# Masks in one load, the gelu average on VectorE, waits reordered on ScalarE, and a new call order on five engines

## The reference

```python
xn = (x - mean(x)) / sqrt(var(x) + 1e-5)
s  = where(mask, xn @ ctx.T * 512**-0.5, -1e30)         # 128 x 128, mask by column
x1 = x + softmax(s) @ ctx
y  = (x1 - mean(x1)) / sqrt(var(x1) + 1e-5)
z  = act_quant(rms_norm(y)) @ weight_quant(w1).T + b1   # 128 x 2048
h  = gelu(silu(z))
l  = (h - mean(h)) / sqrt(var(h) + 1e-5) * g + b
out = x1 + act_quant(rms_norm(l)) @ weight_quant(w2).T + b2
```

## Time and profile before

| | us |
|---|---|
| median of three executions | 419.5 |
| the profiled execution | 421.23 |
| its span, first to last instruction | 419.4 |
| ScalarE busy | 381.8 |
| TensorE busy | 384.0 |
| VectorE busy | 365.9 |
| GpSimd busy | 271.8 |

### The profile page before, as it was taken

How to read it: one execution, slowest core, us unless ns; L and a number is a source line. 1 busy time by engine, 2 the same in 40 slices (tenths; PEclk the granted TensorE clock), 3 DMA queues, 4 the chain that set the end, 5 groups by cost and what they waited for, 6 DMA issues and landing times.

```text
span 419.4 us, 6830 instructions
## 1 busy us (share of the span) xinstructions
PE 384.0 (92%) x1878; PEld 204.7 (49%) x1878; DVE 365.9 (87%) x571; ACT 381.8 (91%) x517; POOL 271.8 (65%) x373
## 2 busy tenths in 40 slices
PE   3899988789999999999999999999999987899996
PEld 2667353535545544544555454554455532344342
DVE  5278669989998989999999999989998789999992
ACT  1497999999999999999999999999999999999960
POOL 5358488764687838764785569585468855477930
PEclk9999998899999999999999999999999996999999
DMA  7998992556755677669668757694654423083484
GB/s 278 409 312 301 359 342 69 153 162 142 211 147 131 188 193 184 103 189 204 155 169 249 190 166 148 199 222 107 174 135 106 91 63 63 2 200 102 87 214 128
DMA packets 110389, 73.87 MB, mean 176 GB/s; under 512 B 87048, under 2 KB 87056, under 8 KB 109584
## 3 DMA queue, kind: packets, MB, share of 16 engines
q1 hardware_dynamic: 110352, 73.43, 65.1%
HBM read 44.05 MB, written 8.39 MB: 125 GB/s over the span
## 4 chain that ended last, share of the span: by engine, by line
issue 25%; ACT 21%; DVE 19%; PE 17%; POOL 13%; DMA 4%; SPq 1%; DVEq 0%; POOLq 0%; ACTq 0%
ACT junk_v L1212 6%; DVE hid L1981 5%; DVE hid L1972 5%; PE z L624 4%; PE acc L649 4%; ACT hid L1201 3%; ACT hid L1207 3%; POOL hid L1618 3%; PE ba L574 3%; ACT junk_l L1223 2%; POOL rstd L1607 2%; DVE am L1986 2%; POOL xc L1563 2%; DVE st L1900 1%; DMA hid<-in_w2T_dram 1%
## 5 line engine op out<-in xcount | busy, mean ns | idle before, releaser
L624 PE MATMUL z<-w1q,q1T 128*128 128x512 f16 x512 | 124.0, 386 | 3.3 <-ACT hid L1201 3.1
L649 PE MATMUL acc<-w2q,q2T 128*128 128x512 f16 x512 | 117.4, 379 | 0.4 <-DMA q2T<-hid 0.4
L1981 DVE SCALAR_TENSOR_TENSOR hid<-hid,rstd,beta 128x2048 f32<-128x2048 f32 x32 | 76.8, 2402 | 6.2 <-POOL rstd L1607 5.9
L624 PEld LDWEIGHTS z<-w1q,q1T 128*128 128x128 f16 x512 | 49.9, 99 | 65.6 <-ACT hid L1201 9.7
L1972 DVE SCALAR_TENSOR_TENSOR hid<-hid,nmu,gain 128x2048 f32<-128x2048 f32 x32 | 79.3, 2480 | 0.4 <-POOL nmu L1599 0.3
L649 PEld LDWEIGHTS acc<-w2q,q2T 128*128 128x128 f16 x512 | 49.8, 98 | 58.2 <-issue 0.9
L1986 DVE TENSOR_REDUCE am<-hid 128x1 f32<-128x2049 f32 x32 | 72.5, 2269 | 0.1
L1201 ACT ACTIVATE hid<-z,fac 128x1024 f32<-128x1024 f32 x64 | 70.7, 1119 | 1.6 <-PE z L629 1.4
L1223 ACT ACTIVATE junk_l<-hid 128x2050 bf16<-128x2050 f32 x32 | 61.1, 1910 | 4.1 <-DVE hid L1981 4.0
L1618 POOL TENSOR_SCALAR hid<-hid,kq 128x2048 f16<-128x2048 f32 x30 | 60.9, 2031 | 4.6 <-DVE kq L1993 3.1
L1212 ACT ACTIVATE junk_v<-hid,gsum 128x2048 bf16<-128x2048 f32 x32 | 63.7, 1990 | 0.1
(11 more groups left out here) (105 smaller groups left out, 572.2 us busy)
## 6 DMA issues: line engine op xcount, KB each, us to landing
ctxT<-in_ctxT_dram SPq DMA_DIRECT2D x32, 256.0 KB, 3.5
xs<-in_x_dram SPq DMA_DIRECT2D x32, 256.0 KB, 3.9
xT<-in_xT_dram SPq DMA_DIRECT2D x32, 256.0 KB, 3.6
ctx<-in_ctx_dram SPq DMA_DIRECT2D x32, 256.0 KB, 3.4
out_dram<-xs SPq DMA_DIRECT2D x32, 256.0 KB, 3.0
hid<-in_w1T_dram SPq DMA_DIRECT2D x4, 1024.0 KB, 10.2
hid<-in_w2T_dram SPq DMA_DIRECT2D x4, 1024.0 KB, 7.8
gain<-in_g_dram SPq DMA_DIRECT2D x1, 1024.0 KB, 11.1
```

The source lines that it names most:

```text
L624: pe.matmul(z_ps[h][:, c * CH:(c + 1) * CH], q1T[:, t % 4, k, :], w1q[:, k, f0:f0 + CH], start=(k == 0), stop=False)
L649: mm = pe.matmul(a, q2T[:, t % 2, c, :], w2q[:, c, :], start=False, stop=(c == FC - 1))
L1981: dve.scalar_tensor_tensor(out=hh, in0=hh, scalar=rstd[:, t:t + 1], in1=beta[:, :], op0=ALU.mult, op1=ALU.add).then_inc(s_l, 1)
```

## The change

Masks: one load of 32 x 128 bytes and one conversion; row t of the mask is picked by multiplying with column t of the identity, broadcast over 128 columns. The matrix of ones is gone.

```diff
-        mask = sb("mask", [1, 2, G, P], U8)
-        maskb = sb("maskb", [P, 2, G, P], BF16)
+        mask = sb("mask", [NT, P], U8)
+        maskb = sb("maskb", [P, P], BF16)
...
+            def load_mask():
+                sp.dma_start(mask[:, :], mask_in[:, :]).then_inc(s_mask, 16)
...
                 if t == 0:
-                    pe.wait_ge(s_const, 1)
-                pe.wait_ge(s_maskb, t // G + 1)
-                pe.matmul(score_ps, ones_b[:, :], maskb[:, t // G % 2, t % G, :], start=True, stop=False)
+                    pe.wait_ge(s_identb, 1)
+                    pe.wait_ge(s_maskb, 1)
+                pe.matmul(score_ps, ident_b[:, t:t + 1].to_broadcast((P, P)), maskb[:, :], start=True, stop=False)
...
+            def mask_bias():
+                pool.wait_ge(s_const, 1)
+                pool.wait_ge(s_mask, 16)
+                pool.tensor_scalar(maskb[0:NT, :], mask[:, :], MASKED, -MASKED, ALU.mult, ALU.add).then_inc(s_maskb, 1)
```

The waits of two steps on ScalarE are listed in another order:

```diff
             def exp_scores(t):
+                wait(act, s_pTp, t - 3)
                 act.wait_ge(s_centred, t + 1)
-                wait(act, s_pTp, t - 3)
...
             def silu(t, h):
-                act.wait_ge(s_z[h], t + 1)
                 act.wait_ge(s_zs, t + 1)
                 if 4 <= t < 8:
                     for c in range(4):
                         act.wait_ge(s_w2q[c], STEPS)
                 if t >= HR:
                     act.wait_ge(s_q2T[t % 2], landed(t - HR, 2))
+                act.wait_ge(s_z[h], t + 1)
```

The gelu average moves from GpSimd to VectorE:

```diff
-            def gelu_mean(t):
-                pool.wait_ge(s_gelu, t + 1)
-                pool.tensor_scalar(nmu[:, t:t + 1], gsum[:, t:t + 1], -1.0 / FF, 0.0,
-                                   ALU.mult, ALU.add).then_inc(s_nmu, 1)
+            def gelu_mean(t):
+                dve.wait_ge(s_gelu, t + 1)
+                dve.tensor_scalar(nmu[:, t:t + 1], gsum[:, t:t + 1], -1.0 / FF, None, ALU.mult).then_inc(s_nmu, 1)
```

At the end, TensorE's `turn_factors(36)` moves from behind `second_product(29, 1)` to between the two halves of tile 29, and on ScalarE `square_l(30)` comes ahead of `variance(31)`:

```diff
             second_product(29, 0)
+            turn_factors(36)
             second_product(29, 1)
-            turn_factors(36)
             second_product(30, 0)
             second_product(30, 1)
             turn_factors(37)
```

More of the change, by code:

```diff
@@ new lines, in _ @@
+            variance(9)
+            copy_probT(15)
+            silu(10, 0)
+            silu(10, 1)
+            mean_term(16)
+            mean_term(17)
+            square_l(8)
+            silu(11, 0)
+            square_x1(14)
+            silu(11, 1)
+            gelu(10)
+            gelu(11)
+            variance(10)
+            square_x1(15)
+            exp_scores(16)
+            variance(11)
+            exp_scores(17)
+            copy_probT(16)
+            silu(12, 0)
+            silu(12, 1)
@@ new lines, in _ @@
+            square_l(9)
+            mean_term(18)
+            mean_term(19)
+            square_l(10)
+            silu(13, 0)
+            copy_probT(17)
+            silu(13, 1)
+            exp_scores(18)
+            square_x1(16)
+            copy_probT(18)
+            exp_scores(19)
+            gelu(12)
+            square_x1(17)
+            gelu(13)
+            variance(12)
+            square_l(11)
+            variance(13)
+            copy_probT(19)
+            silu(14, 0)
+            silu(14, 1)
@@ new lines, in _ @@
+            mean_term(20)
+            mean_term(21)
+            square_l(12)
+            silu(15, 0)
+            square_x1(18)
+            silu(15, 1)
+            gelu(14)
+            gelu(15)
+            exp_scores(20)
+            variance(14)
+            variance(15)
+            exp_scores(21)
+            silu(16, 0)
+            copy_probT(20)
+            silu(16, 1)
+            square_x1(19)
+            square_l(13)
+            square_l(14)
+            mean_term(22)
+            mean_term(23)
@@ L1379, in _ @@
+            copy_probT(21)
+            silu(17, 0)
+            silu(17, 1)
+            exp_scores(22)
+            square_x1(20)
+            exp_scores(23)
+            gelu(16)
+            gelu(17)
+            copy_probT(22)
+            square_x1(21)
+            variance(16)
+            copy_probT(23)
             square_l(15)
-            variance(16)
-            gelu(17)
-            copy_probT(23)
             variance(17)
             silu(18, 0)
+            silu(18, 1)
             mean_term(24)
-            silu(18, 1)
@@ L1458, in _ @@
             silu(27, 0)
+            square_x1(30)
             silu(27, 1)
@@ L2118, in _ @@
-            x1_absmax(8)
             invert_factors(6, 2)
             norm_absmax(2)
+            add_readout(8)
             copy_factors(6)
             gained(3)
-            softmax(10)
+            copy_factors(7)
+            gelu_mean(4)
+            normed(3)
+            output(0)
+            norm_absmax(3)
             add_readout(9)
-            normed(3)
-            copy_factors(7)
-            norm_absmax(3)
-            softmax(11)
+            output(1)
+            gained(4)
@@ L2129, in _ @@
             q2_scale(2, 2)
+            x1_absmax(8)
+            normed(4)
+            gelu_mean(5)
             x1_absmax(9)
-            gained(4)
-            output(0)
+            q1_scale(8, 2)
+            norm_absmax(4)
+            z_scale(8, 2)
+            out_scale(2, 2)
+            softmax(12)
+            invert_factors(8, 2)
+            x_stats(15)
             prob_sum(10)
-            x_stats(12)
-            q1_scale(8, 2)
-            z_scale(8, 2)
-            normed(4)
@@ L2177, in _ @@
+            x_stats(17)
+            add_readout(13)
+            copy_factors(10)
+            softmax(15)
+            gained(7)
+            copy_factors(11)
+            normed(7)
+            output(4)
+            norm_absmax(7)
+            output(5)
+            gelu_mean(8)
+            q2_scale(6, 2)
+            x_stats(18)
+            prob_sum(14)
+            x1_absmax(12)
             x1_absmax(13)
-            norm_absmax(7)
-            q2_scale(6, 2)
-            q1_scale(12, 2)
@@ L2194, in _ @@
             copy_factors(12)
-            output(5)
             gained(9)
+            softmax(16)
+            normed(9)
+            q1_scale(12, 2)
+            output(6)
             copy_factors(13)
-            normed(9)
             add_readout(15)
-            softmax(16)
+            softmax(17)
+            x1_absmax(14)
+            gelu_mean(10)
+            x1_absmax(15)
+            gelu_mean(11)
+            q1_scale(14, 2)
+            gained(10)
+            output(7)
             norm_absmax(9)
-            output(6)
+            prob_sum(16)
@@ L2436, in _ @@
             q2_scale(30, 1)
+            gelu_mean(31)
             round_half0(30)
```

1560 lines of the change are left out of this document (677 added, 883 removed).

## The result

The new kernel takes **435.4 us** (median of four executions, 433.8 to 435.5) against 419.6 us of the kernel before beside it: ratio 1.036, with a 95% interval of 1.034 to 1.039. I had forecast 418.8 us, 411.5 to 426.5. The direction was wrong and the time is outside the range.

What follows compares the result with a forecast made beforehand. ScalarE was taken to bound the kernel from 60 to 400 us, VectorE close behind. The terms 0.4 - 0.4 + 0 - 0.7 = -0.7 us, against the median of 419.5, gave 418.8 us, range 411.5 to 426.5.

Steps and rivals of the forecast that it cites:

- Start to 20 us, +0.4: First 20 us: later column sums and exp(0) give ScalarE 15.5 us idle; plus 0.4 us, bounds -1 and +2.3.
- 20 us to the first gelu, -0.4: From 20 us to the first gelu: new gaps of 3.45 us replace 3.9; minus 0.4 us, between -2.5 and +2.
- w2 lands sooner ... so I cost it at nothing: Load of w2: q1(1) is rounded early, so w2 lands sooner; ScalarE is full from there, so no gain.
- 60 to 400 us: Middle stretch: both engines near full already, so the new orders and small parts cost 0, bounds -4.2 and +7.
- The wait order: silu and exp: the wait listed last precedes the table load, so a late z exposes 1.3 us; early, nothing.
- gelu_mean: 60 to 400 us: 32 instructions move from GpSimd to VectorE, 4.9 us of work that fits in its 21.5 us idle.
- Masks, 0: 60 to 400 us: seven conversions and seven loads go, but GpSimd has 108 us idle there, so 0.
- The end, -0.7: Last tiles: turn_factors(36) goes earlier, so turn and copy no longer hold tile 30; minus 0.7 us, or 0.
- F: Rival on ScalarE's idle time: the new order fills half of 12.8 us, 6.4 us, giving 413; chance 0.27.
- S: Rival, 60 to 400 us: VectorE becomes the bound through gelu_mean's waits for gelu; +7.4 us, 427; chance 0.15.
- T: Rival at the start: TensorE stays slow through the second column sums and readouts; +2.9 us, 422; chance 0.12.
- N: Rival on the wait order: four more table loads meet a late z; 5.2 us on top, 424; chance 0.08.

Runs made afterwards that it cites:

- a_clamps: The new kernel with VectorE's clamps of w2 moved earlier: parts 1 and 2 behind part 0, part 3 behind q2_scale(0, 1); 429.6 us, ratio 1.025.
- b_first: The kernel before with the new masks and the new call order of all five engines up to gelu(1), old wait order; 418.8 us, ratio 1.001.
- a_inv: a_both with invert_factors(28, 2) moved from behind normed(25) to behind out_scale(22, 2); 424.0 us, ratio 1.011.
- a_loads: a_chain with two places of SyncE's order of loads and transposes changed; 423.2 us, ratio 1.009.
- a_zfirst: The new kernel with the waits of silu and exp_scores listed as before, z and the centred scores first; 432.2 us, ratio 1.031.
- a_both: The new kernel with both the old wait order of a_zfirst and the earlier clamps of a_clamps; 426.2 us, ratio 1.016.
- b_zlast: The kernel before with only the waits of silu and exp listed as in the new kernel, z last; 419.5 us, ratio 0.999.
- b_masks: The kernel before with only the masks changed to one load and one conversion; 419.4 us, ratio 0.999.
- b_start: The kernel before with the new masks and the new start on all engines, up to exp_scores(3) on ScalarE; 426.1 us, ratio 1.016.
- a_chain: a_inv with split_factors(28, 2) ahead of gelu_rstd(24, 2), copy_factors(28) ahead of normed(24) and copy_factors(29) ahead of normed(25); 425.9 us, ratio 1.018.
- a_iloads: a_inv with the same two places of SyncE's order changed as in a_loads; 424.3 us, ratio 1.012.
- b_mm: The kernel before with the new masks and gelu_mean moved to VectorE, waits as before; 421.0 us, ratio 1.002.

## Why the prediction was wrong, step by step

- **What bounds the kernel**: right. ScalarE's work stayed the same to 0.1 us, and the change of its idle time (12.7 us) is the change of the span (12.6).
- **The range.** The bounds of the four terms add up to -8.4 and +11.3, which is 411 to 431 us and not the 412 to 428 that I wrote; the range of 411.5 to 426.5 left out the upper part of it. The measured 435.4 is above either.
- **Start to 20 us, +0.4**: the sign was wrong in this trace, 1.8 us less idle, and that is partly luck. I had the column sums end at 11.75 and exp(0) at 15.1; they ended at 11.0 and it began at 13.42. ctxT(1) landed only 0.2 us later than before (first matmul at 7.29, 7.12 before), though it was the fifth load, and both scores ran at the fast 1.13 us:

```profile
7.29 3.75 PE L576 MATMUL ba<-ctxT,neg 128*128 128x256 f32 x8 [7.29 <-DMA ctxT<-in_ctxT_dram]
...
11.86 1.13 PE L565 MATMUL ba<-ctxT,xT 128*128 128x128 f32 x8
...
13.42 0.41 ACT L1041 ACTIVATE prob<-score,nbias 128x129 f32<-128x129 f32 x1 [1.72 <-DVE nbias L1770]
...
16.02 1.97 PE L576 MATMUL ba<-ctxT,neg 128*128 128x256 f32 x8
```

The profile of a_clamps, with TensorE's calls at the same times up to 11.86 us, has the slow scores and slow second column sums:

```profile
11.86 2.04 PE L565 MATMUL ba<-ctxT,xT 128*128 128x128 f32 x8
...
17.90 3.69 PE L576 MATMUL ba<-ctxT,neg 128*128 128x256 f32 x8
```

There ScalarE is idle 15.1 us in the first 20, near the 15.5 that I forecast up to 19.0.

- **20 us to the first gelu, -0.4**: 0 in the trace. The first silu's table load did wait for z, 2.0 us (1.2 forecast). Both terms together, forecast 0, were measured as 0 by b_first (1.001, with the old wait order).
- **"w2 lands sooner ... so I cost it at nothing"**: nothing came of w2's landing. What I did not follow was the next link: when w2 is rounded and clamped, and who waits for that. `silu(4)`'s wait for it stands in the code that I quoted.
- **60 to 400 us, "I take 0", with -4.2 and +7: the step that failed.** It was +14.0, twice the upper bound. I had argued that both engines are near full, so an order can change little; but ScalarE being full before says that the old order fed it in time, and nothing on whether the new one does. I walked the new order as far as the first gelu and took the other 340 us without a walk. The runs put in its place: clamps of w2 late (4.7 us), SyncE's order of loads and transposes at two places (3.3, though nothing on top of a_inv), and the wait order (3.6 once the clamps are mended). With these mended and the factors moved, in a_loads, ScalarE's idle time in this stretch is 5.3 us, against 18.2 in the new kernel and 4.2 before. That the loss was "bounded by nothing but VectorE's reserve" was wrong too. VectorE's amount of work did not bound it: it was idle for 35.9 us of this stretch, 21.5 before. What it did late was the clamps, and TensorE's half clock turned that wait of 6 us into two more late z.
- **The wait order**: the mechanism was right, shown by the rows of a_zfirst and the time from a_clamps to a_both. "Where these are early it costs nothing" was right as well (b_zlast 0.999), but the new order makes them late.
- **gelu_mean**: 4.9 us forecast, 4.2 measured; as costing nothing, right within 0.9 us.
- **Masks, 0**: right (b_masks 0.999).
- **The end, -0.7**: +0.5 in the trace. `turn_factors(36)` did come early, at 417.62 us, but the gap ahead of tile 30's bias product that I had counted as gone is still there. VectorE copies the turned factors only behind `norm_absmax(31)`, and this step I had left out:

```profile
417.46 2.28 DVE L1850 TENSOR_REDUCE am<-hid 128x1 f32<-128x2049 f32 x1
419.65 0.20 DVE L1821 COPY brows<-acc 18x128 bf16<-18x128 bf16 x1
...
420.00 0.38 PE L634 MATMUL acc<-rows,brows 128*128 128x512 bf16 x1 [0.43 <-DVE brows L1821]
```

- **The rivals.** F is false but for the 1.8 us of the start in this trace. S is false: `gelu_mean` waited 0.2 us in all, and VectorE is idle more than before (304.1 of 340 us busy, 318.5 in the earlier trace rows). T did not happen in this execution, where the second column sums took 1.97 us, but in that of a_clamps it did (3.69), at the price of 4.2 us in the first 60, where I had 2.9; it adds to the loss in some executions and does not make it. N came true for its part: five table loads waited for z, and its price of 5.2 us compares with the 3.6 measured once the clamps are mended. It was the right mechanism on the smallest chance, and it came on top of another that I had not named.

Of the 1.38 us drain that the Trainium skill (ScalarE: Activation LUTs, What ACT_TABLE_LOAD costs) adds to a table switch, the new trace shows none either: the load at 86.05 is followed by its ACTIVATE at 87.34, 1.29 us behind it.

**What stays open.** a_loads, the best of the new family, is still 0.9% slower than the kernel before (3.7 us), of which `gelu_mean` may be 0.9; its trace does not point to a single wait for the rest (ScalarE is idle 1.1 us longer than before from 60 to 400 us and 1.3 us behind 400). No version that I ran beats the kernel before by more than can be measured; the nearest are b_first and b_masks, both within 0.4% of it. That `gelu_mean` cost more in the new order than in the old was not tried.

## What to carry to other kernels

When an order of calls is written anew, an engine that is full under the old order is no cover: walk the new order at each place where an engine waits for several others (here a buffer handed over from the weights to the tiles), and look on each engine for a short call behind two long passes. Bisect a large reordering by taking a stretch of all engines' new order up to a common point; one run of that kind (b_first) cleared the start, and a join that cuts through a chain (b_start) shows as a wait of its own. Read a start in the profiles of more than one execution before its gain is believed. Before an edit at one late link is judged, read whether the wait is gone or has only moved to the next link.

## What the runs showed of the hardware that I had not expected

- GpSimd's smallest instructions take eleven times as long beside VectorE's `normed` (two tensor inputs): the L1494 step of the split took 2.21 us in a_inv at 343.98, while the pair at 343.78 ran. In the new kernel it took 0.20 us at 360.95, beside VectorE's reduction (one input). So a chain whose inputs are there early can still be late. The Trainium skill has this rule (SBUF — State Buffer, SBUF: two separate sides): a VectorE instruction with two SBUF inputs and a GpSimd instruction that reads SBUF lock each other out for a whole instruction. These rows agree; I had left it out of the prediction.
- TensorE can start fast or slow with the same calls at the same times. In the profiles of the new kernel and of a_clamps the column sums begin at 7.29 us and the first scores at 11.86 in both; the scores then take 1.13 us in one and 2.04 in the other, and ScalarE is idle 17.3 and 21.5 us up to 60. Of the 13 profiles of kernels with the new start four have the slow first scores (a_clamps, a_zfirst, a_chain, a_iloads), and one, a_clamps, the slow second column sums. The granted clock of the first 20 us reads 1.00 in all 13, so only the durations show it.
- The time of one kernel spreads by some us: a_inv took 422.0 to 425.7 us, a_both 423.6 to 427.9, the kernel before 418.3 to 422.5 in 35 executions beside b_masks, the new kernel 433.8 to 435.5 in four. The start above is one likely part of it; how much was not shown. Another case is in a profile: in that of b_mm, the slowest of its runs (425.9 us), TensorE waited 2.10 us for a load of ctx at 35.9 us, its next scores took 2.02 us instead of 1.11, with the granted clock at 0.73 from 38 to 42 us, and `exp_scores(4)` waited 6.19 us, which the trace of b_masks, with the same calls up to there, has at 2.18.
